# A decoder step in fp32 on one core: softmax sums from ScalarE in self-attention, a new order of TensorE's work in the hybrid attention loop, and filler products in the head

## The reference

```python
x = x + mix(ln(x))       # x @ Wb (rank 64) -> 32 states, butterfly, @ Wc (rank 64), + D * x
x = x + cross(ln(x))     # softmax(x . ctx / 16) over the valid context tokens, @ ctx
x = x + bitlinear_ffn(ln(x))   # ternary weights, rounded inputs, silu(gate) * value, 1024 hidden
x = x + self_attn(ln(x)) # 16 heads of 16, causal
x = x + hybrid(ln(x))    # 16 query heads of 128 on 4 key groups, RMS norm, RoPE, keys = 64 ctx + 256
x = x + moe(ln(x))       # top 1 of 32 masked ternary experts

# self_attn
scores = where(causal, q . k, -inf) / sqrt(16)
probs = softmax(scores)                       # exp(s - max) / sum
out = (probs @ v).reshape(B, S, 256) @ W_out + b_out
# hybrid
scores = (rope(rms(q)) . [rms(k_ctx), rope(rms(k))]) / sqrt(128) + mask
out = (softmax(scores) @ [v_ctx, v]).reshape(B, S, 2048) @ wo
```

## Time and profile before

| | us |
|---|---|
| median of 3 runs | 1186.63 |
| lowest, highest | 1184.10, 1187.51 |
| the profiled execution | 1187.17 |
| its span (first to last instruction) | 1184.3 |
| PE busy in the span | 1041.7 (88%) |
| DVE busy | 877.1 (74%) |
| ACT busy | 653.8 (55%) |
| POOL busy | 326.3 (28%) |

### The profile page before, as it was taken

How to read it: one execution, slowest core, us unless ns; L and a number is a source line. 1 busy time by engine, 2 the same in 40 slices (tenths; PEclk the granted TensorE clock), 3 DMA queues, 4 the chain that set the end, 5 groups by cost and what they waited for, 6 DMA issues and landing times.

```text
span 1184.3 us, 21508 instructions
## 1 busy us (share of the span) xinstructions
PE 1041.7 (88%) x6293; PEld 716.7 (61%) x6301; DVE 877.1 (74%) x2458; ACT 653.8 (55%) x2010; POOL 326.3 (28%) x528
## 2 busy tenths in 40 slices
PE   7788886898999957899999999999999999988395
PEld 5654445676666634565766756657666666666385
DVE  5777774778877767877877878878878788764285
ACT  2777783655555524556556565565565645741262
POOL 3342222111111321312323223223232232101465
PEclk7979997999999978899999999999999999999598
DMA  9710001111111004000000000000000000000731
GB/s 286 251 35 2 1 1 54 55 55 54 53 53 53 19 1 133 26 1 14 1 14 1 1 14 1 5 10 1 16 1 0 14 1 0 15 1 24 263 99 45
DMA packets 38875, 49.58 MB, mean 42 GB/s; under 512 B 5110, under 2 KB 29564, under 8 KB 38528
## 3 DMA queue, kind: packets, MB, share of 16 engines
q1 hardware_dynamic: 36160, 44.16, 12.4%
q0 software_dynamic: 2304, 4.24, 1.0%
q10 hardware_dynamic: 320, 0.15, 0.1%
HBM read 32.70 MB, written 14.78 MB: 40 GB/s over the span
## 4 chain that ended last, share of the span: by engine, by line
PE 47%; ACT 4%; issue 4%; POOL 4%; DVE 3%; DMA 0%; DVEq 0%; ACTq 0%; POOLq 0%
PE PS L1842 41%; POOL out_dram L1417 3%; PE PS L2229 2%; PE PS L2209 2%; ACT arena L1682 1%; POOL tokens_dram L1393 1%; PE PS L2086 1%; DVE arena L823 1%; ACT arena L1691 1%; DVE arena L859 0%; DVE arena L847 0%; ACT early L1618 0%; PE PS L2231 0%; PE PS L2274 0%; PE PS L1852 0%
## 5 line engine op out<-in xcount | busy, mean ns | idle before, releaser
L1842 PE MATMUL PS<-early,arena 128*32 128x128 f32 (+6 forms) x920 | 122.2, 361 | 46.0 <-DVE early L713 23.7
L1842 PE MATMUL PS<-EW,arena 128*128 128x256 f32 (+7 forms) x512 | 121.2, 360 | 16.8 <-DVE small L847 7.3
L1842 PE MATMUL PS<-wq,EW 128*128 128x512 f32 x256 | 125.7, 614 | 6.8 <-DVE arena L823 6.6
L1331 POOL TENSOR_SCALAR small<-small 128x4 f32<-128x4 f32 x64 | 18.6, 291 | 385.2 <-ACT mask L1675 215.5
L1842 PEld LDWEIGHTS PS<-early,arena 128*32 128x32 f32 (+4 forms) x928 | 62.4, 121 | 99.8 <-issue 38.0
L847 DVE CUSTOM_DVE_ANT_0 arena<-PS,kmask 128x128 f32<-128x128 f32 (+3 forms) x256 | 91.4, 389 | 41.4 <-PE PS L1842 35.9
L1691 ACT ACTIVATE arena<-arena,small 128x128 f32<-128x128 f32 (+3 forms) x256 | 119.5, 473 | 0.5 <-DVE small L852 0.3
L1842 PE MATMUL PS<-wo,early 128*128 128x256 f32 x512 | 115.0, 384 | 3.6 <-DVE sinT L900 2.8
L1842 PEld LDWEIGHTS PS<-EW,arena 128*128 128x128 f32 x512 | 83.5, 193 | 43.7 <-issue 23.0
L1842 PEld LDWEIGHTS PS<-wo,early 128*128 128x128 f32 x512 | 98.6, 193 | 17.7 <-DVE sinT L900 3.2
L1682 ACT ACTIVATE arena<-PS 128x512 f32<-128x512 f32 x64 | 38.2, 597 | 114.5 <-PE PS L2209 114.1
(11 more groups left out here) (343 smaller groups left out, 2435.7 us busy)
## 6 DMA issues: line engine op xcount, KB each, us to landing
EW<-in_masksT_dram SPq DMA_DIRECT2D x32, 256.0 KB, 3.5
...
```

The source lines that it names most:

```text
L1842: return pe.matmul(dst, lhs, rhs, start=first, stop=last)
```

## The change

**Head.** The eight bias operations leave DVE in part: DVE keeps three of them (`bias_unit` and two `bias_rest`, spread over n = 4, 5 and 6), ScalarE takes four copies (`bias_round`). `cross_normalise` moves ahead of the weights' scale at n = 4. The rounding pieces come one at a time. PE gets filler products of 128x128 ones (`keep_going`): 8 and 3 at the start, 4 in each n from 4 on (10 at n = 7), 8 in `head_end`.

**Self-attention.** The ones products go. The exps accumulate their rows' sums (`accum_out`), DVE takes the reciprocal of 128x16 sums, spreads them to 128x256 (`self_reciprocals`), PE turns them into bank 6, where the sums stood before, and `self_normalise` copies them from there instead of taking their reciprocal.

**Hybrid.** PE's `outputs(u - 2)` moves behind `turn_query(u + 2)`; `keys` for the next batch move to i = 1, 3 and 4, right behind the first half of the scores; the second half of the turned probabilities goes from DVE to ScalarE; ScalarE's exps move ahead of its other copies; DVE's `square_key` moves to i = 2, 4 and 7, and GpSimd's work on the keys moves with it.

```diff
     dve.wait_ge(d_pv, 4 * b + 2 * m + 2)
     after(dve, d_o, 2 * b + m)
-    dve.reciprocal(dR, PS[:, 6, S:2 * S]).then_inc(d_r, 1)
-    dve.wait_ge(d_r, 2 * b + m + 1)
+    dve.tensor_copy(dRT, PS[:, 6, S:2 * S]).then_inc(d_rt, 1)
+    dve.wait_ge(d_rt, 2 * b + m + 1)
     after(dve, d_y, b)
-    dve.tensor_tensor(dOT[:, m, :], PS[:, 6, 0:S], dR, ALU.mult).then_inc(d_o, 1)
+    dve.tensor_tensor(dOT[:, m, :], PS[:, 6, 0:S], dRT, ALU.mult).then_inc(d_o, 1)
+def self_reciprocals(b, m):
+    dve.wait_ge(d_e, 4 * (4 * b + 2 * m + 2))
+    after(dve, d_r, 4 * b + 2 * m)
+    dve.reciprocal(d_inv, d_sum[:, m].rearrange("p j r e -> p (j r e)")).then_inc(d_r, 1)
+    dve.wait_ge(d_r, 4 * b + 2 * m + 1)
+    after(dve, d_pv, 4 * b + 2 * m)
+    dve.tensor_copy(dR, bc(d_inv.unsqueeze(2), [P, J * P // DH, DH])).then_inc(d_r, 1)
...
         if i == 0:
             if former:
+                self_reciprocals(b - 1, 1)
                 self_normalise(b - 1, 0)
             self_values(b, par)
             ln_apply(*nxt)
         if i == 2:
             if former:
                 self_normalise(b - 1, 1)
+            self_reciprocals(b, 0)
...
-    if i >= XG:
-        dve.tensor_copy(ePT[:, 512:1024], PS[:, 6, :])
...
-        if 2 <= i <= 4 and nxt[0] == HYBRID:
-            square_key(nxt[1], i - 2)
+        if i in (2, 4, 7) and nxt[0] == HYBRID:
+            square_key(nxt[1], {2: 0, 4: 1, 7: 2}[i])
...
+def bias_round(k):
+    act.wait_ge(s_c, mark["unit"] if k == 0 else mark[f"rest{k - 1}"])
+    if k == 0:
+        act.wait_ge(s_l2, 16 * 5)
+        act.activation(biasF, biasF, ACT.Copy, scale=g_unit).then_inc(s_prep, 1)
+        act.wait_ge(s_prep, PIECES + 1)
+    if k < 2:
+        act.activation(biasV, biasF, ACT.Copy).then_inc(s_prep, 1 + k)
+    else:
+        act.activation(biasB, biasF, ACT.Copy, scale=g_any).then_inc(s_prep, 1)
...
+    for i in {5: (1,), 6: (3,), 7: (5,)}.get(n, ()):
+        rounding(i)
...
-    for i in {4: (0, 1), 5: (2, 3), 6: (4,), 7: (5,)}.get(n, ()):
+    for i in {4: (0,), 5: (2,), 6: (4,)}.get(n, ()):
         rounding(i)
+    if n in (4, 5, 6):
+        bias_round(n - 4)
...
+        m, e = i // 2, i % 2
         for r in range(4):
-            act.activation(dP[:, i % 2, r, 0:P], PS[:, r, 0:P], ACT.Exp, bias=d_neg[:, i % 2, 0, r:r + 1])
+            act.activation(dP[:, i % 2, r, 0:P], PS[:, r, 0:P], ACT.Exp, bias=d_neg[:, i % 2, 0, r:r + 1],
+                           accum_out=d_sum[:, m, 0, r, e:e + 1])
             act.activation(dP[:, i % 2, r, P:3 * P], PS[:, r, P:3 * P], ACT.Exp,
-                           bias=d_neg[:, i % 2, 1, r:r + 1]).then_inc(d_e, 1)
+                           bias=d_neg[:, i % 2, 1, r:r + 1],
+                           accum_out=d_sum[:, m, 1, r, e:e + 1]).then_inc(d_e, 1)
...
         if i >= 2 or former:
-            turned_probs(u - 2)
+            turned_probs(u - 2, (i - 2) % 8)
+        exps(u, i)
         if i == 0:
             values(b, par, 0)
-        if i == 1 and more:
-            context(nxt[1])
         if i == 2 and more:
             turned_copy(nxt[1], 1 - par, 2)
-        if i == 3 and more:
-            raw_keys(nxt[1], 1 - par, 2)
+        if i in (1, 3, 4) and more:
+            raw_keys(nxt[1], 1 - par, {1: 0, 3: 1, 4: 2}[i])
         if i == 3 and routed:
             token_copy(b - 2, 7)
         if i == 6 and not more:
             turned_keys(nxt[1], 1 - par, 0)
         if i == 6 and more:
             turned_keys(nxt[1], 1 - par, 1)
-        exps(u, i)
         if further[3]:
             query_squares(u + 3, (i + 3) % 8)
+        if i == 0:
+            values(b, par, 1)
         if i == 7 and routed:
             weights(b - 2)
+        if further[2]:
+            turned_query(u + 2)
         if i >= 2:
             outputs(b, i - 2)
         elif former:
             outputs(b - 1, i + 6)
-        if i == 0:
-            values(b, par, 1)
-        if i == 1 and more:
-            raw_keys(nxt[1], 1 - par, 0)
-        if i == 2 and more:
-            raw_keys(nxt[1], 1 - par, 1)
         if i == 1 and former:
             turned_keys(b, par, 2, 7)
-        if further[2]:
-            turned_query(u + 2)
+        if i == 0 and more:
+            context(nxt[1])
...
+def keep_going(n, at=6):
+    for _ in range(n):
+        product(PS[:, at, 0:P], ones[:, :], ones[:, :])
...
+    if n >= 4:
+        keep_going(10 if n == B - 1 else 4, 4)
...
 def head_end():
+    keep_going(4, 4)
     level_turn(0)
+    keep_going(4, 4)
     pe.wait_ge(s_tern, 2 * (PIECES // 3))
-    pe.wait_ge(s_c, mark["bias"])
+    pe.wait_ge(s_prep, PIECES + 5)
...
-    for summed in range(2):
-        for k in range(2):
-            for r in range(4):
-                weights = d_ones[:, e, :] if summed else dV[:, par, k, 8 * m + 2 * r + e, :]
-                last = product(PS[2 * DH * r:2 * DH * (r + 1), 6, summed * S + k * P:(summed + 1) * S], weights,
-                               dPT[:, i % 2, r, 2 * P * k:2 * P + P * k], e + k + summed == 0, e + k + summed == 3)
+    for k in range(2):
+        for r in range(4):
+            last = product(PS[2 * DH * r:2 * DH * (r + 1), 6, k * P:S], dV[:, par, k, 8 * m + 2 * r + e, :],
+                           dPT[:, i % 2, r, 2 * P * k:2 * P + P * k], e + k == 0, e + k == 2)
+    if e == 1:
+        pe.wait_ge(d_r, 4 * b + 2 * m + 2)
+        for j in range(J):
+            last = pe.transpose(PS[:, 6, S + j * P:S + (j + 1) * P],
+                                dR[:, j * P // DH:(j + 1) * P // DH, :].rearrange("p h d -> p (h d)"), ident[:, :])
     last.then_inc(d_pv, 1)
...
         if further[3]:
             raw_query(u + 3, (i + 3) % 8, pars[3])
-        if i == 2:
-            pe.wait_ge(s_twice, 48 * b + 48)
-        if i >= 2:
-            outputs(u - 2, i - 2, par)
-        elif former:
-            outputs(u - 2, i + 6, 1 - par)
...
             turn_query(u + 2, (i + 2) % 8)
+        if i == 2:
+            pe.wait_ge(s_twice, 48 * b + 48)
+        if i >= 2:
+            outputs(u - 2, i - 2, par)
+        elif former:
+            outputs(u - 2, i + 6, 1 - par)
+        if i == 0:
+            pe.wait_ge(e_vr, 2 * b + 2)
+        if i == 1 and former:
+            turn_keys(b, 2, 7)
+        if i == 2 and former:
+            pe.wait_ge(e_kc, 3 * b + 3)
+        if i == 2 and routed:
+            token_turn(b - 2, 7)
```

106 lines of the change are left out of this document (50 added, 56 removed).

## The result

Over 20 runs of each the changed kernel takes 1177.15 us against 1185.41, a ratio of 0.993 with an interval from 0.9915 to 0.9945: some 8 us faster. The forecast was 1172 in a range of 1161 to 1190, 14.6 us under the 1186.63 that stood for the kernel before. One of the changed kernel's 20 runs took 1364.21 us at a granted clock of 0.73, and the ratio leaves it out.

A forecast was written before the change was run, and what follows sets the result against it. Bounds: in self-attention the circle of scores, maxima and exps, in the hybrid a full PE, in the head ScalarE's queue. Head -4, self-attention +2, hybrid -13 from 1187.17 gave 1172.2, 1172 against the median 1186.63; range 1161 to 1190 us.

The forecast's parts named there:

- The circle in self-attention: Self-attention: scores, maxima, exps and again scores set every step's pace; 7.01 us a step, 28.04 a batch against 27.28.
- The read: Self-attention, ACT: each of eight accumulator reads per step adds 0.10 us to the circle; as a rival 0.145, chance 0.10.
- The first batch: Self-attention's first batch: 25.99 us before, taken as four steps of 7.01, so +2.05 us.
- the clock rival: Self-attention: idle time ahead of the scores lowers PE's clock, +10 us per hit a batch; total 1197, chance 0.10.
- The end of self-attention: After self-attention's last steps: both reciprocals shrink by 1.33 us and half the output products go; -4.5 us.
- 13.7 us is all that reordering can win there: Hybrid: PE is busy 500.34 of 514 us, so its idle time bounds the gain over six and a half batches.
- the stretch up to the first addition: Hybrid's start, from its first query product to the first batch's addition to X; -2 us.
- the 17 that I had called the most: Hybrid: gain at most 17 us, from all labelled waits and a fifth of the first window's idle time.
- the last batch: Hybrid's last batch: -1 us from the new order.
- Step 7: Hybrid: DVE's slack of 1.66 us becomes a lag of about one, felt by the turned queries; +0.3 us net a batch.
- this shrinks by 1.18 each time: Head, n = 4 to 6: PE's waits of 1.77 and 1.30 us for ScalarE's copy shrink with one rounding ahead, not two.
- may win back the slow sets: Head: filler products may hold PE's clock and bring two slow mix sets back to speed, 2 x 1.7 us.

The follow-up runs named there:

- third_key_earlier: The changed kernel with DVE's square_key of the hybrid's third key block at i = 6 instead of 7; ratio 1.0105, 21 us slower than the changed kernel.
- last_batch_as_before: The changed kernel with outputs back in their old place in the last hybrid batch only (i = 6 and 7); ratio 0.9891, -4.6 us against the changed kernel.
- head_alone: The kernel before with only the head's part of the change (bias rows, roundings, fillers); ratio 0.9996 (0.9978 to 1.0014).

## Why the forecast was right, and where it wasn't

**The circle in self-attention: right.** A step of 7.01 forecast, 6.94 to 7.02 found; a batch 28.04, found 27.89. The read came out at 0.09 instead of 0.10 (3.34 less 2.60, by eight). PE is at the scores before the last exp, as the argument needed. One wait of PE for L713 stayed, 0.74 us once a batch, where I had said none; it doesn't lengthen the circle, since PE waits for the exps behind it anyway.

The first batch was mis-sized: +3.3 against +2.05. Its steps took 6.62, 6.84, 6.02 and 6.51 us before and 7.91, 7.58, 6.76 and 7.03 after. I had set the batch to four bare circles, but its first two steps were longer than the circle before too, and the eight reads of each step came on top, 0.5 to 0.74 a step. The rest is clock: scores and masks of the first step took 0.56 us more than before, at the lower level, behind a wait of PE of 2.80 us (1.88 before). That is the clock rival, for one step. In the six batches behind it, with 22.77 of 27.89 us busy and waits up to 1.7 us, the clock was 1.00, apart from some 3 us at the start of the first of them, behind a wait of 2.29, which lengthened no step. Two traces, of the changed kernel and of third_key_earlier, show what went with a fall in self-attention and the hybrid: behind 18 of the 19 gaps in PE's work of 2.3 us and more the clock was at the lower level or fell to it within 2 us (the exception is the 2.79 us before 1038.73 in the changed kernel); behind those of 1.2 to 1.7 it never did. Like the head, self-attention has PE busy for 79%, which was the rival's argument; its waits are shorter.

**The end of self-attention: right in kind, 1.2 us too high.** Forecast -4.5, found -3.3. Both reciprocals did shrink to a copy. The outputs and turns took 3.5 us where I had 2.4, since all of them ran at the lower level; before, the last of that work (428.40 to 429.24) had run at the upper.

**The hybrid: right in sign, and in its sum by luck.** Three of its terms were off: two won more than forecast, one lost.

The first is the bound, "13.7 us is all that reordering can win there". The six batches lost 12.8 us, while PE's idle time in them fell only from 13.0 to 10.7, not to the 5 or less that I had named as the sign; the other 10.5 us went out of its busy time, with the same number of products (2030 and 2032). Counting each product from its start to the next one's start places them. From the last turned probabilities' start to the next scores' start it is 0.11 us in all 48 steps after; before it was 0.57 in 16 of them, where the wait is labelled 0.30, and 0.41 in eight, where the list of waits names nothing. That is 10.3 us. The scores right behind (224 or 96 columns) ran 399 and 297 ns before and 354 and 262 after, 3.9 us by their starts. The waits ahead of the turned queries took 4.0 back, step 7's for the most part, and some 2 us are spread over other groups. So a wait of 0.30 us had cost 0.46 from start to start, because the products on either side no longer overlapped, and more in the products behind it; that was the price that I had read off the label.

The second is the stretch up to the first addition: -2 forecast, -7.5 found, with 2.1 us less idle time and 5.4 less busy time. What it won wasn't broken down. With it the hybrid won 20.3 us before its last batch, more than the 17 that I had called the most; that bound doesn't follow from its own terms either, as 11.5 and a fifth of 13.6 are 14.2.

The third is the last batch, -1 forecast and +6.4 found. I had taken its order to be like the others', and did not follow the waits for the routing (`f_lg`) past the moved outputs, though the order of the queue was there to be read. last_batch_as_before settles it.

The hybrid part has five moves (outputs, keys, copies, exps, `square_key`), and no run has them one by one. That the waits for L1682 went is seen; which of the moves it took for that was only argued.

**Step 7: right, a little too small.** About 1 us forecast, 1.6 found. The reduction is 0.71 us of it, as I had it; the 0.26 that DVE waits for GpSimd in the middle of the key's operations I had not.

**The head: wrong.** -4 forecast; 0.9996 with 1.8 per mil either way. Two steps failed. The first is "this shrinks by 1.18 each time": PE's two waits for ScalarE's copy were 1.77 and 1.30 us before and are 1.92 and 1.16 after. One rounding did leave its place ahead of the copy, but bias copies came to stand there instead, which I had put later in ACT's queue (ACT at n = 4, behind one rounding that ends at 54.08):

```profile
53.98 0.71 ACT L1523 ACTIVATE early<-early,small 128x512 f32<-128x512 f32 x1
54.72 0.63 ACT L1526 ACTIVATE early<-early 128x512 bf16<-128x512 f32 x1
55.25 0.58 ACT L1473 ACTIVATE arena<-PS 128x512 f32<-128x512 f32 x1
```

The second is "may win back the slow sets". In this execution both came at the upper level, 1.99 us each instead of 3.78 and 3.68, and that, not shorter waits, is why cross attention's turns of batches 4 to 6 came 1.6, 3.6 and 2.1 us sooner (1.1, 2.7 and 1.4 forecast). But I had read two slow sets as caused by the two waits ahead of them, and in other executions of the same code others are slow. Of the 3.6 us only 0.9 were left at the gate product, with eight fillers at the lower level right ahead of it. Where the front did win 3 us in head_alone, ScalarE's wait for the next layer's weights took them back; the forecast had named transfers at the start, but those of the mix's batches.

**The chances** had 0.80 on faster by more than 0.3%, and faster it was, by 0.7%. The summed gain was too large by the last batch (7.4 us off) and the head (some 3.5 off), and too small by the hybrid's other batches (some 8 off in the profile). That these nearly cancelled is luck; the medians gave 6 of the 14.6 us less than forecast.
